# Four sandwiched layers on one core: weight halves split during the preceding stage, value products in pairs of rounds, the eighth round's sum shared by two engines, the last group's sums moved among the next stage's tiles

## The reference

```python
x = x + ln(L0_attn(ln(x)))   # a small recurrent network: long convolution by FFT, 4 blocks
x = x + ln(L0_ffn(ln(x)))    # silu-gated FFN, quantised weights repeated 4 times, rank-2 LoRA
x = x + ln(L1_attn(ln(x)))   # causal attention, 32 heads of 32, 8 key/value heads
x = x + ln(L1_ffn(ln(x)))    # projection plus a mixture of 8 LoRA experts

# L1_attn
q = x @ Wq;  kv = x @ Wkv                     # 32 query heads, 8 key and value heads, head size 32
scores = q @ k.T  (causal: -inf above the diagonal)
weights = softmax(scores / sqrt(32));  ctx = weights @ v
return ctx @ Wo + bo
```

## Time and profile before

| what | value |
|---|---|
| median of three executions | 2188.68 us |
| profiled execution, its own time and its span | 2191.21 us, 2189.3 us |
| granted TensorE clock, mean over the span | 0.969 |
| PE busy | 2027.6 us, 93% |
| DVE busy | 1421.0 us, 65% |
| POOL busy | 1019.1 us, 47% |
| ACT busy | 947.1 us, 43% |
| DMA, share of the 16 engines | 33.2% on the main queue |

### The profile page before, as it was taken

How to read it: one execution, slowest core, us unless ns; L and a number is a source line. 1 busy time by engine, 2 the same in 40 slices (tenths; PEclk the granted TensorE clock), 3 DMA queues, 4 the chain that set the end, 5 groups by cost and what they waited for, 6 DMA issues and landing times. The chain is left out here.

```text
span 2189.3 us, 30704 instructions
## 1 busy us (share of the span) xinstructions
PE 2027.6 (93%) x10444; PEld 1450.0 (66%) x10444; DVE 1421.0 (65%) x3274; ACT 947.1 (43%) x1979; POOL 1019.1 (47%) x882
## 2 busy tenths in 40 slices
PE   5889986999999989989999999999988999999998
PEld 4555445788888879755555555555554687888887
DVE  7877667677777763386665667567768577654433
ACT  5645685233333333135554555455556433332211
POOL 1444586444444420028875577666886133220000
PEclk9999998999999999999999999999998999999999
DMA  6400276122222157412224622322223275554432
GB/s 192 172 1 19 102 250 221 39 78 78 77 78 77 68 190 260 113 44 65 63 76 106 194 71 68 89 64 78 61 74 122 83 260 175 177 168 149 135 123 99
DMA packets 146475, 249.65 MB, mean 114 GB/s; under 512 B 27166, under 2 KB 77214, under 8 KB 146192
## 3 DMA queue, kind: packets, MB, share of 16 engines
q1 hardware_dynamic: 135312, 227.77, 33.2%
q10 hardware_dynamic: 11008, 19.93, 2.9%
HBM read 139.89 MB, written 76.02 MB: 99 GB/s over the span
## 5 line engine op out<-in xcount | busy, mean ns | idle before, releaser
L2180 ACT ACTIVATE c_P<-PS 128x512 f32<-128x512 f32 (+3 forms) x768 | 358.4, 495 | 331.9 <-PE PS L2009 311.2
L1991 PE MATMUL PS<-c_K,c_Q 96*128 96x512 f32 (+3 forms) x768 | 276.2, 370 | 20.0 <-DVE cst L2335 12.4
L2009 PE MATMUL PS<-c_Q,c_K 97*128 97x512 f32 (+3 forms) x768 | 281.8, 380 | 7.3 <-DMA c_Q<-c_mT 5.4
L2442 POOL TENSOR_TENSOR c_S<-c_S,c_P 128x2048 f32<-128x2048 f32 (+3 forms) x94 | 272.7, 2901 | 8.6 <-ACT c_P L2180 0.2
L2009 PEld LDWEIGHTS PS<-c_Q,c_K 97*128 97x128 f32 x768 | 147.5, 194 | 171.7 <-ACT c_P L2180 93.1
L2331 DVE TENSOR_REDUCE cst<-PS 128x1 f32<-128x512 f32 x256 | 176.0, 688 | 95.3 <-PE PS L1991 94.8
L213 POOL TENSOR_TENSOR maskw<-maskw,mhalf 128x1 f32<-128x1 f32 x64 | 37.3, 582 | 359.2 <-DVE maskw L171 346.5
L1991 PEld LDWEIGHTS PS<-c_K,c_Q 96*128 96x128 f32 x768 | 150.1, 196 | 74.9 <-DVE cst L2335 35.2
L2024 PE MATMUL PS<-c_P,c_V 128*32 128x512 f32 (+3 forms) x1536 | 168.9, 512 | 16.6 <-POOL c_P L2419 8.3
L2335 DVE CUSTOM_DVE_ANT_0 PS<-PS,maskw,cst 128x128 f32<-128x128 f32 (+3 forms) x256 | 143.0, 558 | 60.3 <-PE PS L1991 42.9
L2335 DVE CUSTOM_DVE_ANT_0 PS<-PS,maskw 128x128 f32<-128x128 f32 (+3 forms) x256 | 126.5, 504 | 70.1 <-PE PS L1991 67.8
(11 more groups left out here) (306 smaller groups left out, 4769.7 us busy)
## 6 DMA issues: line engine op xcount, KB each, us to landing
a_xin<-in_x SPq DMA_DIRECT2D x32, 512.0 KB, 4.2
d_x<-scr SPq DMA_DIRECT2D x32, 512.0 KB, 4.9
c_Q<-c_qh SPq DMA_DIRECT2D x240, 64.0 KB, 2.0
scr<-a_xin SPq DMA_DIRECT2D x16, 512.0 KB, 5.7
b_xn<-scr SPq DMA_DIRECT2D x16, 512.0 KB, 5.6
b_x<-scr SPq DMA_DIRECT2D x16, 512.0 KB, 4.7
scr<-b_x SPq DMA_DIRECT2D x16, 512.0 KB, 2.6
scr<-b_y SPq DMA_DIRECT2D x16, 512.0 KB, 3.0
```

Source lines behind the costliest of these rows:

```text
L1991: e.matmul(bank[:, 0:hi - lo], self.Q4[0:96, 4 * (o % 3) + g, 128 * t:128 * t + 128], self.K4[0:96, HEADS[o % 8], lo:hi], start=True, stop ...
L2009: e.matmul(self.k.bank(i % 3)[:, 0:hi - lo], self.K4[0:97, HEADS[o % 8], 128 * kt:128 * kt + 128], self.Q4[0:97, 4 * (o % 3) + g, lo:hi], ...
L2180: e.activation(self.P[:, R % 3, g, 0:hi - lo], self.k.bank(i % 3)[:, 0:hi - lo], ACT.Exp, scale=SCALE).then_inc(self.exp_s.s, 1)
L2442: e.tensor_tensor(S[:, :, 512 - n:512], S[:, :, 512 - n:512], P[:, :, 0:n], ADD).then_inc(self.psum_s.s, 1)
```

## The change

1. **Weights from stage B.** Fourteen weights (`PRE`: two of keys, eight of queries, Wo rows 0 to 3) are loaded, split and stored during stage B, half a weight at a time, 28 pieces. A piece takes three of B's chunk steps: ACT issues the load (256 KB); in the next step ACT copies (128x512) and POOL subtracts; in the next ACT issues the store of both parts (512 KB) to `pre_d`. Stage C then loads a half with both parts (512 KB) into a ring of three pieces, and the ACT copies, DVE and POOL subtractions of jobs' weights in C are gone. SP issues half 1 of the next job and half 0 of the one behind it in slot `slots[15] + 2` of a job, behind any placing and finishing of the same slot. PE waits for a half at steps 0 and 4.
2. **PV in pairs.** In twelve of the sixteen groups (all but `SINGLE`) PE makes the PVs of two rounds together at odd `r`; the sum of `s == 20` moves to 21, right behind such a pair.
3. **Round 7** (`BOTH`): POOL adds `g` 0 and 1, DVE adds `g` 2 and 3, in groups 0 to 14 except where DVE had it already.
4. **Wo:** rows 0 to 3 come from `pre_d` by DMA straight into `c_xth` and `c_xtl`; rows 4 to 7 are split by ACT and POOL, no longer by DVE.
5. **The end of C:** the last three `pe_zero` chunks go between and behind the last PVs; the sums of the last group (group 31 in the code's count of half groups), their evacuation and their way through memory move into D's tiles 1 and 2.

The core of the diff:

```diff
+    def act_pre(self, e, t, c):
+        p, step = self.pre_step(t, c)
+        if step == 0:
+            if p > 0:
+                e.wait_ge(*self.pre_out(p))
...
+        if step == 1:
+            e.wait_ge(*self.pre_in(p + 1))
+            e.copy(self.pre[:, 0, :], self.raw).then_inc(self.pre_hi.s, 1)
+        if step == 2:
+            e.wait_ge(*self.pre_lo(p + 1))
+            e.dma_start(self.k.pre_d[p], self.pre[:, :, :].bitcast(F32)).then_inc(self.pre_out.s, 16)
...
+    def pool_pre(self, e, t, c):
+        p, step = self.pre_step(t, c)
+        if step == 1:
+            e.wait_ge(*self.pre_hi(p + 1))
+            e.tensor_tensor(self.pre[:, 1, :], self.raw, self.pre[:, 0, :].bitcast(F32), SUB
...
+SINGLE = (5, 8, 14, 15)
+BOTH = 7
...
                 if S in self.place_at:
                     self.sp_place(e, *self.place_at[S])
-                for n, q in self.split_at.get(S, ()):
-                    if q == 3:
-                        self.sp_w(e, n + 2)
...
+                if S in self.next_at:
+                    self.sp_w(e, self.next_at[S] - 1, 1)
+                    self.sp_w(e, self.next_at[S], 0)
...
+        if q in (0, 4):
+            e.wait_ge(*self.wld[q // 4](self.set_of(n) + 2))
         if c == 0:
-            if part == 0:
-                e.wait_ge(*self.wlo_s(self.pieces(self.piece_of(n))))
...
-                if g == 1 and S > 8:
-                    self.pe_pv(e, *divmod(S // 4 - 2, 12))
+                R = S // 4 - 2
+                if g == 1 and R >= 0:
+                    if R // 12 in SINGLE:
+                        self.pe_pv(e, *divmod(R, 12))
+                    elif r % 2:
+                        self.pe_pv(e, *divmod(R - 1, 12))
+                        self.pe_pv(e, *divmod(R, 12))
...
-                if s == 20 and o not in BY_ROUND:
+                if s == 21 and o not in BY_ROUND:
                     self.pe_sum(e, 2 * o)
+        self.then.pe_zero(e, 5)
         self.pe_pv(e, 15, 10)
+        self.then.pe_zero(e, 6)
         self.pe_pv(e, 15, 11)
+        self.then.pe_zero(e, 7)
...
-                for n, q in self.split_at.get(S, ()):
-                    if n + 1 not in POOL_W.values():
-                        self.low_w4(e, n + 1, q)
+                if s in (35, 36) and (o, BOTH) not in LAST and o < 15:
+                    self.dve_both(e, o, s - 33)
...
+                if r == BOTH + 1:
+                    e.wait_ge(*self.both_s(2 * o + 2))
+                gs = slice(0, 2 if r == BOTH else 4)
+                e.tensor_tensor(S[:, gs, 512 - n:512], S[:, gs, 512 - n:512], P[:, gs, 0:n], ADD).then_inc(self.psum_s.s, 1)
...
-            if u == 1:
-                self.before.dve_rec(e, 31)
...
-            if u + 1 < 2 * NT:
+            if u == 1:
+                self.before.dve_rec(e, 31)
+            if 0 < u < 2 * NT - 1:
                 self.dve_lo(e, u + 1, 0)
```

More of the change, by code:

```diff
@@ L1525 @@
 HEADS = (0, 2, 4, 6, 1, 3, 5, 7)
+PRE = [(name, n, half) for name, n in [("wk", 0)] + [("wq", j) for j in HEADS] + [("wk", 1)] + [("wo", c) for c in range(4)]
+       for half in range(2)]
 LEAD = 12
@@ L1641, in tables @@
                 self.place_at[place[0]], self.place_at[place[1]] = (n, 0), (n, 1)
-                soon = n + 1 < len(JOBS) and JOBS[n + 1][1][0] < slots[15] + 8
-                for q in range(4):
-                    self.split_at.setdefault(slots[15] + 2 + q // (2 if soon else 1), []).append((n + 1, q))
+                self.next_at[slots[15] + 2] = n + 1
         self.bank_of, self.held_by = {}, {}
@@ L1670, in tables @@
                     keeps.append(kept)
-                if o not in BY_ROUND and s == 20:
+                if o not in BY_ROUND and s == 21:
                     keeps.append(turn(o, 49))
@@ L1678, in turn_bank, with set_of, last_of, turn_of @@
         return self.k.bank(self.bank_of[o, a])
[L1680 to L1690, removed]
     @staticmethod
-    def piece_of(n):
-        return 2 if n < 2 else n + 1
+    def set_of(n):
+        return max(n - 1, 0)
     @staticmethod
-    def pieces(n):
-        return n + 1 if n < 7 else 4 * n - 17
+    def last_of(m):
+        return m + 1 if m else 1
+    @staticmethod
+    def turn_of(m):
+        return m // 2 if m < 4 else m - 2
+    def piece(self, m, half):
+        return self.pair[half] if m in (1, 3) else self.ring[(2 * self.turn_of(m) + half + 1) % 3]
+    def stored(self, m, half):
+        what = JOBS[m + 1][0] if m else "K0"
+        return PRE.index(("wk", 0 if m == 0 else 1, half) if what in ("K0", "K2", "K3") else ("wq", HEADS[what % 8], half))
     @staticmethod
@@ L1704, in job_bank, with w @@
         return 7 if JOBS[n][1] else 5 + 2 * part if n else 6 + part
-    def w(self, n):
-        return (self.wh2, self.wl2) if n in (3, 5) else (self.wh, self.wl)
+    def w(self, n, c):
+        piece = self.piece(self.set_of(n), c // 4)
+        return tuple(piece[:, a, 128 * (c % 4):128 * (c % 4) + 128] for a in range(2))
     def low(self, n, part):
@@ L1736, in summed, with sp_wv @@
         return self.sum_s(E + 1 - sum(2 * b <= E for b in BY_ROUND))
[L1739 to L1743, removed]
-    def sp_wo(self, e, c):
[L1747 to L1752, removed]
+    def sp_wv(self, e, n):
+        if n == 1:
+            e.wait_ge(*self.before.u2_s(192))
+        e.dma_start(self.raws[n], self.k.io["wv"][:, 128 * n:128 * n + 128].rearrange("(c p) n -> p c n", p=128)
+                    ).then_inc(self.wld[n].s, 16)
@@ new lines, in sp_w @@
+    def sp_w(self, e, m, half):
+        if m >= len(JOBS) - 1:
+            return
+        e.wait_ge(*self.wld[half](m + 1))
+        if m == 0:
+            e.wait_ge(*self.before.pre_out(len(PRE)))
+        if m == 2 and half == 0:
+            e.wait_ge(*self.wlo_s(1))
+        if m == 2 and half == 1:
+            e.wait_ge(*self.qmm_s(2 * self.last_of(0) + 2))
+        if m == 3:
+            e.wait_ge(*self.qmm_s(2 * self.last_of(1) + 2))
+        if m > 3:
+            i = self.turn_of(m) - 2 + half
+            e.wait_ge(*self.qmm_s(2 * self.last_of((0, 2)[i] if i < 2 else i + 2) + 2))
+        e.dma_start(self.piece(m, half)[:, :, :].bitcast(F32), self.k.pre_d[self.stored(m, half)]).then_inc(self.wld[half].s, 16)
@@ L1876, in sp @@
                 self.sp_place(e, n, part)
-        self.sp_w(e, 5)
-        for n in (2, 3):
-            for part in range(2):
-                self.sp_place(e, n, part)
-            self.sp_w(e, n + 4)
+        self.sp_w(e, 2, 1)
+        self.sp_place(e, 2, 0)
+        self.sp_w(e, 3, 0)
+        self.sp_w(e, 3, 1)
+        self.sp_place(e, 2, 1)
+        self.sp_w(e, 4, 0)
+        self.sp_place(e, 3, 0)
+        self.sp_w(e, 4, 1)
+        self.sp_w(e, 5, 0)
+        self.sp_place(e, 3, 1)
         self.sp_place(e, 4, 0)
@@ L1904, in sp @@
         self.then.sp_second(e)
-        for step in range(5):
-            self.sp_finish(e, 31, step)
-        for i in range(2):
-            e.wait_ge(*self.ctx[i](16))
     def pe_x(self, e, u):
@@ L2585, in sp @@
                 self.sp_org(e, 0)
+                for step in range(4):
+                    self.before.sp_finish(e, 31, step)
             if (u, 0) in CHUNKS:
@@ L2599, in sp @@
                 self.sp_org(e, CHUNKS.index((u, 1)))
+            if u == 2:
+                self.before.sp_finish(e, 31, 4)
+                for i in range(2):
+                    e.wait_ge(*self.before.ctx[i](16))
             if u == NT:
@@ L2713, in pe @@
                     self.pe_out(e, u, half)
-                if u == 0 and half == 0:
+                if u == 1 and half == 0:
                     self.before.pe_sum(e, 31)
```

212 lines of the change are left out of this document (107 added, 105 removed).

## The result

The changed kernel takes 2176.38 us (median of 13 executions, 2165.72 to 2182.73) against 2187.39 for the kernel before (13, 2184.06 to 2191.76): ratio 0.9943, interval 0.993 to 0.9957. It is faster, by 11 us and not by the 40 that were forecast, and its executions spread over 17 us instead of 8.

What follows compares the result with a forecast made beforehand. The prediction took PE, busy 2027.6 us, as the bound. Its terms, mostly steady groups' −31.2, summed to −41.7 from the profiled 2191.2, so 2149.5; for the median, 2.5 lower, it gave 2148, range 2132 to 2172.

Steps and rivals of the forecast that it cites:

- Pairs: Stage C, twelve groups: joining PVs saves PE 0.30 us per switch, 2.1 us a group; bounds 0 and 2.1.
- The wait at slot 1: Stage C, six groups: PE's wait for an exponential goes as POOL is relieved, 1.0 us each; bounds 0 and 1.0.
- The stretch behind the jobs: Stage C, behind a group's job steps: DVE loses 2.4 us of subtractions, so 0.8 us of PE's waits go.
- the 42.6: Steady groups of stage C: expected at 42 to 43 us if the forecast's steps hold.
- DVE and POOL set the pace: Rival, stage C: the pairs' 2.1 us in twelve groups turn into waits; about 2173 us, chance 0.14.
- Halves that come late: Groups 4, 5, 8, 9: late weight loads cost 8 us, 3.8 at K2's step 4; net −1, bounds −9 and +6.
- 1 us each: Jobs 7 and 11: the late weight's wait overlaps one already paid for the row of maxima, leaving 1 us each.
- Stage B: Stage B: copies waiting for loads delay silus, +2 us for the whole stage; bounds 0 and 56.
- the rival of 2202: Rival, stage B: each of 28 pieces holds up a silu, 56 us instead of 2; 2202 us, chance 0.06.
- Prologue, groups 13 and 14: Prologue −2.5 us from less DVE work; group 13 −3 from POOL's subtractions moved; group 14 0.
- The end: Junction of C and D: chunks fill waits, −5 us; tile 2's low part behind the reciprocal, +2; net −3.
- Group 15: Group 15 of stage C: loses DVE's splitting of four Wo rows, −3 us; bounds 0 and −4.

Runs made afterwards that it cites:

- e3: The changed kernel with all values' products made one by one in all sixteen groups, the rest of the change kept: 2172.09 us, ratio 0.9918 to the kernel before.
- e5: The changed kernel with the two pairs behind the job steps made two slots earlier: 2167.38 us, ratio 0.9894 to the kernel before.
- e4: The changed kernel with round 7 added by POOL alone again, DVE's two sums of it gone: 2185.31 us, ratio 0.9981 to the kernel before.
- e2: The changed kernel with values' products of slots 17 to 29 made one by one again in the paired groups: 2163.45 us, ratio 0.9891 to the kernel before.
- e7: The changed kernel with single products in slots 17 to 29 and half of round 8 on DVE too: 2165.34 us, ratio 0.9888 to the kernel before.
- e8: The changed kernel with the next weight's half 1 and the row of maxima ahead of finishing and placing on SP: 2151.29 us, ratio 0.9831.

## Why the prediction was wrong, step by step

**Pairs: the step that failed.** The forecast took "2.1 us in each of twelve groups" from them; against e3, where the sums of slot 21 stand behind a product too, they gave 0.02. The price of a switch held where job steps lie: 0.28 us a pair measured, 0.30 forecast. Behind the jobs the step failed at "the exponential that reuses its buffer comes just behind the pair; two more scores cover it": ACT stands 1.5 to 2.2 us there, and instead of saving 0.6 us the two pairs cost 1.1 (e3, e5). Where job steps lie ACT stands as long, and yet the pairs save:

```profile
1542.57 0.87 ACT L2252 ACTIVATE c_P<-PS 128x384 f32<-128x384 f32 x2 [1.62 <-PE PS L2100]
```

So the cover comes, it seems, from the jobs' own matmuls, which PE can make without ACT; no run tests this apart. Two further terms came out near their size. The wait at slot 1 went (1.01 to none): with no pairs but with POOL's relief, e3 has 0.19 us of it left, and e4 prices the relief. The stretch behind the jobs fell by 0.88 us (14.20 to 13.32 in e3) where 0.8 were forecast for DVE's relief; but in e3 the sums also join a product there, one switch of about 0.3, so DVE's own part is nearer 0.6.

**The next bound was not priced.** Repairing the stretch by 1.1 us (e2, e5) shortened the group by only 0.2: slots 0 to 15 grew by 0.6, the wait for POOL's last sum, and with POOL relieved the maxima came late (e7). First POOL's chain up to the group's last sum and behind it DVE's maxima hold a group at 44.1 to 44.2, so the 42.6 were not to be had by pairing. The rival "DVE and POOL set the pace" (2173) came nearest, since it takes the pairs' gain away whole; its place was right and its cause half: ACT's ring of buffers first, and POOL and DVE only behind it.

**Halves that come late.** The mechanism was right, and the first size by luck; SP, ACT and PE of the changed kernel:

```profile
1149.08 0.40 PE L2067 MATMUL PS<-c_K,c_Q 96*128 96x512 f32 x1
1149.25 0.59 SPq L1874 DMA_DIRECT2D c_Q<-c_qh  x1
1149.94 1.03 SPq L1814 DMA_DIRECT2D c_w<-pre_d  x2
...
1153.51 0.80 PE L2043 MATMUL PS<-c_xth,c_w 128*128 128x512 f32 x1 [4.03 <-DMA c_w<-pre_d]
1188.39 0.80 PE L2043 MATMUL PS<-c_xth,c_w 128*128 128x512 f32 x1 [4.02 <-DMA c_w<-pre_d]
...
1196.65 0.39 PE L2085 MATMUL PS<-c_Q,c_K 97*128 97x512 f32 x1
...
1380.25 0.25 ACT L2214 CAST c_mT<-PS 32x128 fp32r<-32x128 f32 x1
...
1389.81 0.53 SPq L1881 DMA_DIRECT2D c_Q<-c_mT  x1
...
1393.95 0.80 PE L2085 MATMUL PS<-c_Q,c_K 97*128 97x512 f32 x1 [6.22 <-DMA c_Q<-c_mT]
```

K2 waits 4.03 us where 3.8 were forecast, but two errors of about a microsecond cancel in it. PE had come to the step at 1149.48 (1153.51 less the wait), 0.5 us before the load went out at 1149.94, where the forecast had the load 0.8 us ahead of the step; and the load landed 3.5 us after its issue, not 4.6. The median of all such loads is 4.2, for a second one issued right behind lands later (4.4 here):

```profile
c_w<-pre_d SPq DMA_DIRECT2D x34, 512.0 KB, 4.2
b_raw<-in_wq ACTq DMA_DIRECT2D x16, 256.0 KB, 2.9
```

"1 us each" held for job 7: it waits 4.02, and the row's wait of 2.94 behind it is gone (the score at 1196.65). It was mis-sized for job 11. In K3's group the row of maxima, ready at 1380.5, is issued at 1389.8, behind the placing and two weights: 6.22 us instead of 2.15 before. I counted one wait as covering the other and so as nearly free, but the row stands behind the weights on SP. By e8 late issue on SP held 24 us of these groups: 13.5 in the waits named here, and the rest, by the granted clock of groups 4 and 9, in matmuls at the lower clock. I had 2 us for the clock. Two sums were wrong besides: three stalls of 3.8 and 2 us are 17.4, so the upper bound of this term was +8 and not +6, and 2149.5 less 2.5 is 2147, not 2148; neither decides anything.

**Stage B** cost nothing; the rival of 2202 is out. From its first silu to its last it takes 440.8 to 444.8 us in the twelve profiles that have the pieces, 442.7 and 445.1 in the two that do not. The 256 KB load takes 2.9 us, not the 4.6 of the whole weight that I took, so the copy runs as soon as ACT comes to it, and the silu behind keeps its 3.35 us after the one before:

```profile
630.18 0.56 ACT L1315 ACTIVATE b_g<-PS 128x460 f32<-128x460 f32 x1 [1.92 <-PE PS L1136]
630.63 0.58 ACT L1254 COPY b_xT<-PS 128x512 f32<-128x512 f32 x1
631.10 0.63 ACT L1278 CAST b_pre<-b_raw 128x512 fp32r<-128x512 f32 x1
633.53 0.55 ACT L1315 ACTIVATE b_g<-PS 128x460 f32<-128x460 f32 x1 [1.80 <-PE PS L1156]
```

**Prologue, groups 13 and 14** came out within 1.5 us of their terms. **The end** gave 1.3 behind the last exponential instead of 3, though the wait that I feared at tile 2 stayed at 0.25 us behind a reciprocal at 1722.59:

```profile
1722.59 0.25 DVE L2394 RECIPROCAL cst<-cst 128x16 f32<-128x16 f32 x1 [6.37 <-DMA cst<-sum_d]
...
1723.44 0.50 PE L2707 MATMUL PS<-c_xth,d_xh 128*128 128x512 f32 x1 [0.25 <-DVE d_xl L2870]
```

Group 15 gave 4.6 instead of 3. The two belong together: three chunks of about 1.4 us left group 15 for the place behind its last score. Without this move group 15 gave about 0.3 and the end about 5.5, so each term was mis-sized by some 2.5 us and only their sum (−5.9 against −6) came out.

## What to carry to other kernels

Joining short matmul runs saves the switch, but whoever reuses their inputs waits for the later one: count the buffers of the ring before the slots. When one queue issues everything, a load that is moved must be followed past every transfer that stands ahead of it in the same slot, and two waits at one place must both be priced, since mending one only uncovers the other (−6 and −4.5 apart, −24 together). And a saving is worth no more than the distance to the next bound: look for the second-longest chain before summing gains.

## What was not expected of the hardware

DVE's two sums of round 7, two inputs each, took 1.30 and 0.91 us; the like sums of rounds 4 and 5, with POOL idle, 0.69. DVE and POOL of the changed kernel, group 12, and of the kernel before (L2264, L2397), group 11:

```profile
1562.37 0.69 DVE L2332 TENSOR_TENSOR c_S<-c_P 128x512 f32<-128x512 f32 x1
1570.79 1.30 DVE L2338 TENSOR_TENSOR c_S<-c_S,c_P 128x512 f32<-128x512 f32 x1
1572.22 0.91 DVE L2338 TENSOR_TENSOR c_S<-c_S,c_P 128x512 f32<-128x512 f32 x1
...
1569.14 2.39 POOL L2490 TENSOR_TENSOR c_S<-c_S,c_P 128x1024 f32<-128x1024 f32 x1
1571.49 1.09 POOL L2467 TENSOR_SCALAR_AFFINE_SELECT c_P<-c_P 128x512 f32<-128x512 f32 x1
...
1522.06 0.41 DVE L2264 TENSOR_TENSOR c_wl<-c_raw,c_wh 128x256 fp32r<-128x256 f32 x1
1522.80 1.18 DVE L2264 TENSOR_TENSOR c_wl<-c_raw,c_wh 128x256 fp32r<-128x256 f32 x1
1522.41 1.29 POOL L2397 TENSOR_TENSOR c_cH<-c_cH,c_cS 128x512 f32<-128x512 f32 x1 [0.94 <-DMA c_cS<-rec_d]
```

POOL's sum ends at 1571.53 and DVE's first 0.56 us later; the mask ends at 1572.58, DVE's second 0.55 later. The Trainium skill's rule of an exclusive port pair ("SBUF — State Buffer", section "SBUF: two separate sides") agrees with this row by row. The mask, which began while DVE's first sum was under way, paid too: 1.09 us where masks take 0.63 in the median. I had read the mean of the earlier trace rows as speaking against the rule, and that was a wrong reading: of those four subtractions three took 0.41 us and one, which met POOL's product, 1.18, ending 0.28 us after it. They are also half as wide as round 7's sums, so 0.6 us was no estimate of these. The price was about 0.8 us a group on DVE, since each sum met only the end of a POOL operation.
